# Attention stage of an AdaLN block: first scores computed in pairs on the two halves of the array, projections moved to free halves of banks

## What is computed

```python
x = _layernorm(hidden_states, ln1_g, ln1_b)
Q = jnp.einsum('bsd,dhr,hre->bhse', x, q_U, q_V) + q_b[None, :, None, :]
...
scores = jnp.einsum('bhse,bhte->bhst', Q, K) * scale
scores = jnp.where(causal[None, None], scores, -1e9)
attn = jax.nn.softmax(scores, axis=-1)
ctx = jnp.einsum('bhst,bhtd->bhsd', attn, V)
ctx = ctx.transpose(0, 2, 1, 3).reshape(B, S, D)
attn_out = ctx @ out_U @ out_V + out_b
```

## Time and profile before

| | us |
|---|---|
| median of 3 runs (lowest, highest) | 707.95 (707.64, 711.16) |
| profiled execution: its own time | 706.39 |
| its span | 704.6 |
| first reduction of first scores starts | 42.66 |
| first second scores start | 67.91 |
| stage after attention begins (first MLP product) | 381.42 |

### The profile page before, as it was taken

The page is one execution under the profiler, slowest core; times in us unless marked ns, Lnnn a source line. Parts: engine busy times, 40 slices in busy tenths (PEclk is TensorE's granted clock), DMA queues, the critical chain, the costliest instruction groups (busy, mean ns, idle before and its releaser), DMA issues.

```text
span 704.6 us, 15442 instructions
## 1 busy us (share of the span) xinstructions
PE 633.6 (90%) x5389; PEld 416.6 (59%) x5389; DVE 447.6 (64%) x1346; ACT 409.1 (58%) x720; POOL 301.7 (43%) x480
## 2 busy tenths in 40 slices
PE   4977899999999999999978886999998999999997
PEld 3543444444444544444434575766766999999993
DVE  5749887878788776767742878777673222222227
ACT  4432667676676767666666565676434555555550
POOL 4232424243442524232313438766771545455452
PEclk9999999999999999999999998999899999999999
DMA  9552332443343344332463511211236777777769
GB/s 212 189 177 74 118 102 87 144 138 113 109 153 102 126 140 136 131 106 72 132 189 108 143 36 50 81 51 50 70 96 197 205 239 222 221 224 225 234 209 322
DMA packets 86125, 100.97 MB, mean 143 GB/s; under 512 B 13008, under 2 KB 68216, under 8 KB 85952
## 3 DMA queue, kind: packets, MB, share of 16 engines
q1 hardware_dynamic: 76896, 87.19, 40.3%
q0 software_dynamic: 4544, 9.45, 3.7%
q10 hardware_dynamic: 4608, 3.35, 1.8%
HBM read 60.28 MB, written 37.57 MB: 139 GB/s over the span
## 4 chain that ended last, share of the span: by engine, by line
PE 53%; DVE 14%; DMA 9%; ACT 8%; SPq 6%; issue 5%; POOL 4%; POOLq 0%; ACTq 0%; DVEq 0%
PE ps_pv L1293 9%; PE ps_r L1478 7%; PE ps_s L1468 6%; DVE row_max L1669 6%; PE ps_r L1248 5%; PE ps_r L1245 4%; DMA arena<-slots_d 4%; PE ps_pv L1364 4%; PE ps_s L1276 3%; POOL slots_d L910 3%; PE ps_r L1223 2%; PE ps_s L1272 2%; PE ps_s L1372 2%; ACT arena L1081 2%; DMA arena<-in_w_mod 1%
## 5 line engine op out<-in xcount | busy, mean ns | idle before, releaser
L1669 DVE TENSOR_REDUCE row_max<-ps_r 128x1 f32<-128x384 f32 (+3 forms) x384 | 206.9, 595 | 63.1 <-PE ps_r L1248 61.8
L989 ACT ACTIVATE arena<-ps_s 128x1024 f32<-128x1024 f32 (+1 forms) x192 | 159.3, 881 | 70.8 <-PE ps_s L1276 69.8
L1248 PE MATMUL ps_r<-arena 128*128 128x384 bf16 (+3 forms) x512 | 118.7, 303 | 0.0
L956 POOL DMA_INDIRECT y_d<-arena,target x78 | 74.9, 960 | 87.7 <-DVE arena L1878 75.5
L1245 PE MATMUL ps_r<-later_q,ident_b 128*128 128x128 bf16 (+1 forms) x384 | 91.4, 244 | 22.0 <-DVE row_max L1669 15.8
L1245 PEld LDWEIGHTS ps_r<-later_q,ident_b 128*128 128x128 bf16 x384 | 35.9, 97 | 84.1 <-DVE row_max L1669 42.4
L1874 DVE TENSOR_TENSOR arena<-ps_r,arena_early 128x256 f32<-128x256 f32 x39 | 16.6, 425 | 108.2 <-PE ps_r L1478 108.2
L1293 PE MATMUL ps_pv<-arena 128*32 128x512 f32 (+3 forms) x1024 | 83.3, 443 | 0.1
L910 POOL DMA_INDIRECT slots_d<-arena,slots x64 | 65.5, 1023 | 18.2 <-issue 18.2
L1276 PE MATMUL ps_s<-arena 51*128 51x256 bf16 (+3 forms) x512 | 59.9, 298 | 0.0
L1478 PEld LDWEIGHTS ps_r<-arena 128*128 128x128 f32 x480 | 58.2, 192 | 1.5
(11 more groups left out here) (236 smaller groups left out, 1129.1 us busy)
## 6 DMA issues: line engine op xcount, KB each, us to landing
arena<-in_ew SPq DMA_DIRECT2D x30, 514.0 KB
ctx_d<-ctx_raw SPq DMA_DIRECT2D x32, 256.0 KB, 3.1
arena<-q_d SPq DMA_DIRECT2D x64, 102.0 KB
arena<-k_d SPq DMA_DIRECT2D x64, 96.0 KB
arena<-slots_d SPq DMA_DIRECT2D x39, 132.0 KB, 3.1
arena_early<-in_ew SPq DMA_DIRECT2D x9, 514.0 KB
arena<-y_d SPq DMA_DIRECT2D x8, 512.0 KB, 6.0
q_d<-arena_early SPq DMA_DIRECT2D x8, 384.0 KB, 2.9
```

What stands on the lines that cost most here:

```text
L956: pool.indirect_dma_start(y_d[:], bass.IndirectOffsetOnAxis(ap=target[:, k, c:c + 1], axis=0), res[:, k, c, :], None).then_inc(put[k], 16)
L989: act.activation(dst, src, ACT.Exp, scale=SCALE).then_inc(exp_done, 1)
L1248: mm = pe.matmul(bnk[:, k * keys:(k + 1) * keys], q_st[b % 2][:, g, j, i * P:(i + 1) * P], k_st[b % 2][:, g, j // 2, 0:keys], start=False, ...
L1669: dve.reduce_max(row_max[:, m % 2, js[0] % 2, j:j + len(js), i], src, AXIS.X).then_inc(max_taken, 1)
```

## The change

In `s1` two units (even and odd heads) run as a pair: masks as four products of 64 rows, scores as products of 48 rows, the even head on rows 0 to 47 into one bank of the ring, the odd head on rows 64 to 111 into the next. `q_st` keeps two slots in place of four, so the zero rows, their stores and the two ACT writes go. Q and K (b > 0), V and U (b < 6) leave the ring for columns 256 to 511 of banks 2 and 3 of `ps_s2`, M for a corner of bank 3; they are written behind the fourth exponential of a step and emptied by ACT behind the sixth. PE's order is woven anew in six slots, each a pair of `s1`, one unit of `s2` and a part of `context`. `layer_norm` is called after units 1, 3, 7 and 9 with half as much each time. In steps -3 to -1 an fp32 product of 512 columns into `ps_pv`, which nothing reads, stands before each pair.

```diff
@@ ring_order @@
-        units(m, 0, 1)
-        one(n, "O")
-        units(m, 2, 3)
-        if 0 <= m - 1 < NG:
-            order.append(("M", m - 1))
-        units(m, 4, 5)
-        one(n, "T", "K", "V")
-        units(m, 6, 7)
-        one(n, "Q")
-        units(m, 8, 9, 10, 11)
...
+        units(m, 0, 1, 2, 3, 4, 5)
+        one(n, "T")
+        units(m, 6, 7)
+        one(n, "O")
+        units(m, 8, 9)
+        one(n, *(name for name in "QKU" if not beside(name, batch_at(n, AT[name]))))
+        units(m, 10, 11)
@@ SyncE: load_stack @@
-                                sp.dma_start(q_st[b % 2][HALF * half:HALF * half + QROWS, g, half:JH:2], q_rows[0:QROWS, heads, :])\
+                                sp.dma_start(q_st[b % 2][HALF * half:HALF * half + SROWS, g], q_rows[0:SROWS, heads, :])\
@@ ScalarE: start and step @@
-                    for stack in q_st:
-                        act.activation(stack[:].rearrange("p g j s -> p (g j s)").bitcast(F32), zeros[:, 0:1].to_broadcast([P, GROUPS * JH * S // 2]), ACT.Copy)\
-                            .then_inc(q_zeroed, 1)
...
-                        if b is not None:
-                            empty_qk(b, 1)
-                        if batch_at(n, V_AT) is not None:
-                            empty_v(batch_at(n, V_AT))
-                        if batch_at(n, Q_AT) is not None:
-                            empty_qk(batch_at(n, Q_AT), 0)
                         if has:
                             exp_unit(n, 4)
                             exp_unit(n, 5)
+                        if batch_at(n, Q_AT) is not None:
+                            empty_qk(batch_at(n, Q_AT), 0)
                         if b is not None:
+                            empty_qk(b, 1)
+                        if b == 0:
                             qk_middle(b, 1)
+                        if batch_at(n, V_AT) is not None:
+                            empty_v(batch_at(n, V_AT))
+                        if batch_at(n, AFTER_T_AT) is not None:
+                            empty_after(batch_at(n, AFTER_T_AT))
@@ TensorE @@
+                    def place_of(name, b):
+
+                        if not beside(name, b):
+                            bank(name, b)
+                            return home(name, b)
+                        n = GROUPS * b + AT[name]
+                        pe.wait_ge(small_copied, 4)
+                        wait(pe, act_emptied, beside_until(n))
+                        wait(pe, max_copied, min(n + LAG, NG))
+                        wait(pe, exp_done, NS2 * n + 4)
+                        return home(name, b)
...
+                    def fill_in(n):
+
+                        if -LAG <= n < 0:
+                            pe.matmul(ps_pv[:], ident[:], w_fc1[:], start=True, stop=True)
...
-                            diag = bnk[:, 0:len(js) * keys].rearrange("p (j s) -> p j s", j=len(js))[:, :, keys - P:keys]
-                            pe.matmul(diag, ident_b[:], later_q[:].unsqueeze(1).to_broadcast([P, len(js), P]), start=True, stop=False,
-                                      skip_group_check=True)
+                            banks = [bank("S", NS1 * m + u + half)[:, 0:len(js) * keys].rearrange("p (j s) -> p j s", s=keys) for half in range(2)]
+                            for stationary, at in ((lower_q, keys - P), (upper_q, keys - HALF)):
+                                for half in range(2):
+                                    whole = slice(HALF * half, HALF * half + HALF)
+                                    near = ident_h[whole].unsqueeze(1).to_broadcast([HALF, len(js), HALF])
+                                    pe.matmul(banks[half][:, :, at:at + HALF], stationary[whole], near, start=(at == keys - P), stop=False,
+                                              skip_group_check=True)
                             for k, j in enumerate(js):
-                                mm = pe.matmul(bnk[:, k * keys:(k + 1) * keys], q_st[b % 2][:, g, j, i * P:(i + 1) * P],
-                                               k_st[b % 2][:, g, j // 2, 0:keys], start=False, stop=True, skip_group_check=True)
-                            mm.then_inc(s1_done, 1)
+                                for half in range(2):
+                                    rows = slice(HALF * half, HALF * half + SROWS)
+                                    mm = pe.matmul(banks[half][:, k, :], q_st[b % 2][rows, g, j // 2, i * P:(i + 1) * P],
+                                                   k_st[b % 2][rows, g, j // 2, 0:keys], start=False, stop=True, skip_group_check=True)
+                                    if k == len(js) - 1:
+                                        mm.then_inc(s1_done, 1)
@@ VectorE: layer_norm @@
-                        second = u == 7
+                        second = u > 4
+                        quarters = {1: (0, 1), 3: (2, 3), 7: (0, 1), 9: (2, 3)}[u]
...
-                            for i in (2, 3) if second else (0, 1):
-                                normalise(b, i)
+                            normalise(b, quarters[0] // 2 + 2 * second)
```

203 lines of the change are left out of this document (116 added, 87 removed).

## The result

The changed kernel takes **724.78 us** (median of 4 runs, 720.86 to 730.53) against 708.34 for the kernel before (4 runs beside it). The ratio is 1.0231, 95% interval 1.0145 to 1.0316: slower by 1.4 to 3.2%. The forecast was 691.8 with a range of 678 to 705; the time lies above rival (d)'s 716. The profiled execution, the longest of the four, took 730.53 us (span 728.8, mean granted clock 0.931 for 0.980).

What follows compares the result with a forecast made beforehand. TensorE's one queue starves VectorE and ScalarE in turn; with its stream halved, VectorE bounds. Gains 0.7 + 4.4 + 4.5 + 4.4 + 0.7 + 1.5 = 16.2 from 706.4 give 690.2, median 691.8, range 678 to 705.

Steps and rivals of the forecast that it cites:

- rival (d): Stops leave TensorE idle; if lighter stream drops the clock in ordinary steps, 716 at one step in five; chance 0.11.
- The halved stream: First scores in TensorE: pairing frees 3,584 columns, 1.6 us a step, 51 us over 32 steps, but VectorE comes next.
- The wait for the root: VectorE waits 2.4 us for POOL's h_rstd, queued behind K's remainder, in steps 5, 9, 13 and 17; bounds 0, 2.7.
- I take the clock as full: TensorE's clock in the new steps: stays full as the steps before show 1.00, so nothing is added.
- The wait for the sums: Reciprocals, once per four-step cycle: VectorE waits 1.4 us for SP's load of the sums; bounds 0 and 2.5.
- Full cycles of 37.2 without the two waits: Four attention steps: VectorE's 34.4 us, 2.2 where TensorE is late, 0.6 for exponentials; 41.0 with root and sums waits.
- The fourth cycle at 35.8 and the fifth at 33.4: Later cycles without the norm, the fifth also without T, Q, K and loads: gains of 4.4 and 4.5 us.
- rival (b): Bank hand-over, a pair needing two of three banks, costs 0.4 us more per step over 30 steps: 704; chance 0.15.
- The beginning (4.4) and ahead of step 0 (1.5): From 67.91 us to first reciprocals 64.3 us for 68.7, gaining 4.4; smaller ring waits less unread products gain 1.5 earlier.
- The unread products: 18 products in steps -3 to -1: lengthen the steps by 1.7 us and the first cold ones by about 1.
- The end: Last steps: steps 27 and 28 gain 2.1 us, step 30's wait for maxima gives about 1.4 back: 0.7 gained.
- rival (a): Waits for root and sums are covered, 4 x 2.4 + 5 x 1.2 less: about 676; chance 0.17.

Runs made afterwards that it cites:

- e17: e16 with every unit of first scores streaming its score products twice, the first time unread; 712.67 us, 26.6 more.
- e1: Changed kernel with POOL computing the root for h_rstd ahead of K's remainder; 708.65 us, ratio to before 0.9982.
- e14: e9 with the root for h back behind K's remainder, as in the changed kernel; 716.67 us, 19.0 more than e9.
- e4: Kernel before with h_rstd computed one step later and two tiles normalised after unit 1, giving a similar VectorE stop; 720.69 us, ratio 1.0182.
- e9: e6 with SP storing the context rows of step n - 2 first in its step; 697.7 us, ratio 0.9796.
- e5: e1 with SP loading the sums ahead of the step's eight stack loads; 712.17 us, 3.5 more than e1.
- e15: e13 with each half of a pair taking its bank by itself; 688.65 us, 5.4 less than e13.
- e13: e9 with the two halves of each pair of first scores issued one after the other; 694.05 us.
- e2: Changed kernel without the 18 unread products of steps -3 to -1; 719.52 us, 5.3 less than the changed kernel.
- e6: e5 without the 18 unread products; 703.77 us, 8.4 less than e5.
- e10: e5 with the context stored first, that is e9 with the 18 unread products; 706.04 us, 6.1 less than e5.
- e12: e9 with SP's late loads for the second part spread over steps 27 to 32; 693.66 us, 4.0 less than e9.
- e16: e15 and e12 together: banks taken singly and late loads spread; 686.08 us, ratio to before 0.9697.
- e3: Changed kernel with every pair of first scores streaming its score products twice, the first time unread; 730.65 us.

## Why the prediction was wrong, step by step

- **The halved stream (1.6 us a step freed): right**, and more central than I made it. "It is not the gain, because VectorE comes next" fails: giving the stream back cost 26.6 us (e17), and both consumers still waited for TensorE.
- **The wait for the root: right in place and length** (2.4 forecast, 2.52 measured, four times), **wrong in price.** The step that failed is "I take the clock as full". A stop costs 4.0 to 4.7 us (e1, e14), so 16 to 19 in all for the 9.6 in the sum. I had read before's 1.00 as proof for the new steps; e4 shows why that row couldn't carry it: with the longer stream TensorE stands 1.44 us at such a stop and keeps 1.00. The Trainium skill ("TensorE: Matmul & The Clock Gate", section "A second HAM failure mode: psum-queue depth-cycling") warns of idles between groups of matmuls that cycle through PSUM banks. The trace agrees in part: the idles between pairs alone lowered the clock only for short pieces (e9: 0.98 to 1.00 in the cycles, 0.86 from 292 to 304 us, where no idle is above 0.65), and most of the loss came with longer idles on top. Rival (d) had the mechanism, a stop that leaves TensorE idle and the low clock behind it, but put its price on ordinary steps.
- **The wait for the sums: right** as far as it could show. It stood at 0.6 and 3.7 us in the changed kernel and 1.8 to 2.6 in e1 (1.4 forecast). Removing it alone brought nothing (e5), since ScalarE's wait for the store of the context lay beside it. That wait is the step I didn't have: `empty_ctx` moved two places up ScalarE's queue, and the sum has no term for what it waits for on SP. Both with the unread products are 11.0 us (e1 to e9).
- **Full cycles of 37.2 without the two waits: right in size.** e9 has 37.4, 38.2 and 37.0. One term was too small: the output's products, put at 0.4, keep the addition waiting 0.6 to 1.6 us in e9 (0.6 to 3.5 in e1), so another must have been too large; no run tells which.
- **The fourth cycle at 35.8 and the fifth at 33.4: too short.** The 35.8 holds 1.6 for the second wait, which e9 doesn't have, so e9's 37.3 stands against 34.2 and its 36.9 against 33.4: wrong by 3.1 and 3.5. The term "VectorE works 4.9 less" was taken as a gain, with 1.9 given back; the cycle hardly got shorter though VectorE's share did. That TensorE and the banks pace it is rival (b)'s mechanism, argued from e15 and e17 and not isolated for this cycle.
- **The beginning (4.4) and ahead of step 0 (1.5): wrong in sign.** In e1, without stops, the first reciprocals come 5.8 us later than before, 2.6 of it a wait for the sums; in e9, without either wait or unread products, still 2.9 later. Taking banks singly is worth 7.6 us up to there (e13 to e15). I had written down that "a pair can be written when the first half of the pair before it is reduced" and taken it as no cost, because VectorE would have the second half to reduce; ahead of step 0, with nothing else in the slots, it doesn't cover the masks, the products and the way to VectorE.
- **The unread products (1.7 and 1 us): too cheap.** They cost 5.3 to 8.4 (e2, e6 to e5, e9 to e10), and only a part is explained.
- **The end (0.7 gained): wrong in sign**, 2.5 us lost by the last two distances. TensorE's wait for the late maxima grew from 2.83 to 6.15 us (before 391.55, released by ScalarE's `max_rows`), where "about 1.4 back" was in the sum. The cause is SP's block of loads in step 27, as the prediction suspected; spreading it was worth 2.6 to 4.0 (e12). The block stands in the kernel before too, and what spreading brings there was not run.
- **What would show it wrong** did: clock below 0.97 between 68 and 340 (0.84 to 0.91), reductions waiting 55 us, cycles of 44.

The clock is the step whose price is isolated, but not the largest part of the miss of 33.0 us. The stops cost 16 to 19 us for the 9.6 in the sum, 6.5 to 9.4 too little. The remainder lies in the other terms. With root, sums and store moved and no unread products, e9 takes 697.7, and this is not where the forecast stood: without its two waits the forecast is rival (a)'s 676, some 22 us lower. (The unread products, 2.7 in the sum, are gone in e9 too, so the gap is rather 25.) In e9's trace the 22 are the first reciprocals (139.5, forecast 128.3 without the first wait), 3.1 and 3.5 in the fourth and fifth cycle, 3.5 at the end and 1.0 in the full cycles. Banks taken singly and spread loads win back 12 of them (e16, 686.1); for the other 10 the cause stays open.

## What to carry to other kernels

When work moves up one engine's queue, write down what that instruction waits for on every other queue, and what stands in that queue ahead of it; here the place of one root in POOL's queue was worth 16 us, and that of one store in SP's 6. A clock that reads 1.00 is a fact about the stream that was measured: when an edit lightens TensorE and adds a stop, price the stop with a stretch at the low clock behind it, and check the clock column against the times of the matmuls themselves. With few banks, hand over in the smallest unit that the consumer takes, whatever unit the producer issues.

## What the runs showed of the hardware that I had not expected

- A stop of 2.5 us on VectorE was followed by the low clock where the stream was the new one (changed kernel, four of four; e14, three of four), and not where it was the old one or the new one filled up (e4, e3). Of the stretches read one by one, the low clock came behind idles of TensorE of 2.00 to 2.59 us (changed kernel, e1, e14) and once behind 1.61 and 0.79; it stayed at 1.00 behind 1.44 (e4), 1.67 (e3), 1.50 and 1.59 (e1, before 225.98 and 265.48), 1.63 (e14, before 195.84) and once behind 1.62 and 0.80 (e14). Nor does it need a long idle: in e9 `context`'s first part took 1.93 us at 298.97 behind idles of 0.24 to 0.65 us. These rows give no rule.
- Two half-height groups of matmuls overlap when they are issued one group after the other: 0.33 us for a pair either way (e9, e13), where 0.46 is what they would take in a row.
- The clock column can be wrong for a stretch: it reads 1.00 from 42 to 68 us in e9 and 0.50 in e6, yet the masks take 0.29 us in both, and `context`'s first part in step 1 began at 85.19 and 85.61 us.
